# Attention stage in units of four tiles: running sum weighted on ScalarE, plain transposes in the residual, scattered rows based on GpSimd

## The reference

```python
def _L0_attn_ref(x, W_proj, A, Bp, D, W_delta, b_delta):
    delta, Bs, Cs, residual = jnp.split(x @ W_proj.T, 4, axis=-1)
    delta = jax.nn.softplus(delta @ W_delta.T + b_delta)
    dA = jnp.exp(delta * A[0, 0]) * Bp[0, :, 0]
    dB = jnp.cumsum(delta * Bp[0, :, 0], axis=1)
    uC = jnp.sum(x * Cs, axis=1, keepdims=True)
    Csum = jnp.sum(Cs, axis=1, keepdims=True)
    return dA * uC + dB * Csum + residual * D

x = x + 0.5 * ffn(layernorm(x))    # 32 experts, top 1, 640 slots each
x = x + _L0_attn_ref(layernorm(x))
x = x + 0.5 * ffn(layernorm(x))    # the same weights
```

## Time and profile before

| | |
|---|---|
| median of 3 runs | 1527.41 us (1524.95 to 1527.49) |
| the profiled execution | 1527.63 us |
| its span, first to last instruction | 1525.8 us |
| instructions | 31260 |
| mean granted TensorE clock over the span | 0.933 of full speed |
| busy share of the span | PE 85%, DVE 81%, ACT 71%, POOL 44% |
| HBM traffic over the span | 174 GB/s |

### The profile page before, as it was taken

One profiled execution on the slowest core, in us unless ns is written; L12 is line 12 of the kernel. 1 busy time (PEld: TensorE's weight loads), 2 busy tenths in 40 slices (PEclk: granted clock), 3 DMA queues, 4 the chain that ended last, 5 costly groups with the idle time before them and its releaser, 6 DMA issues. The chain is left out here.

```text
span 1525.8 us, 31260 instructions
## 1 busy us (share of the span) xinstructions
PE 1298.1 (85%) x10212; PEld 1229.3 (81%) x10215; DVE 1239.9 (81%) x3385; ACT 1088.4 (71%) x2343; POOL 675.9 (44%) x778
## 2 busy tenths in 40 slices
PE   5555029999999999799999999987639999999996
PEld 4334019999999999599888888986529999999996
DVE  8999408999999998388999999999837777777775
ACT  6778117777777775589889888886537777777773
POOL 0577752444334444222254554544633344434443
PEclk8877559999999999899999999999859999999999
DMA  9979546766667661921111232111144444444440
GB/s 325 346 271 378 198 160 206 234 223 227 232 207 234 218 212 61 291 72 35 36 62 53 73 102 84 47 60 53 54 144 128 125 148 129 145 147 130 148 130 25
DMA packets 149776, 234.74 MB, mean 154 GB/s; under 512 B 24333, under 2 KB 124390, under 8 KB 147568
## 3 DMA queue, kind: packets, MB, share of 16 engines
q1 hardware_dynamic: 121968, 188.24, 38.2%
q0 software_dynamic: 27648, 44.50, 8.5%
HBM read 128.51 MB, written 136.48 MB: 174 GB/s over the span
## 5 line engine op out<-in xcount | busy, mean ns | idle before, releaser
L1034 PE MATMUL ps<-xs,ws 128*128 128x320 f32 x3072 | 469.6, 311 | 2.2 <-issue 2.2
L1034 PEld LDWEIGHTS ps<-xs,ws 128*128 128x128 f32 x3072 | 454.7, 189 | 8.2 <-issue 8.2
L859 POOL DMA_INDIRECT slots_and_rows<-x x160 | 161.5, 1010 | 238.1 <-DVE x L976 198.5
L859 POOL DMA_INDIRECT out<-x x160 | 157.8, 987 | 236.5 <-DVE x L966 153.8
L1034 PE MATMUL ps<-ws,hs 128*128 128x256 f32 x1920 | 260.6, 289 | 1.3 <-DVE hs L955 1.3
L1034 PEld LDWEIGHTS ps<-ws,hs 128*128 128x128 f32 x1920 | 239.0, 190 | 1.7 <-DVE hs L955 1.7
L898 ACT ACTIVATE x<-x 128x256 f32<-128x256 f32 x320 | 165.0, 594 | 64.8 <-DMA x<-slots_and_rows 49.2
L880 ACT CAST xs<-ps 128x512 fp32r<-128x512 f32 (+1 forms) x192 | 98.3, 513 | 130.4 <-PE ps L1027 130.4
L987 DVE TENSOR_TENSOR hf<-ps,sg 128x320 f32<-128x320 f32 x256 | 124.6, 487 | 81.6 <-ACT sg L919 77.7
L948 DVE TENSOR_TENSOR xs<-ps,xs 128x512 fp32r<-128x512 f32 (+1 forms) x192 | 113.5, 592 | 72.5 <-ACT xs L880 72.5
L373 POOL DMA_INDIRECT slots<-x,slot x128 | 132.9, 1038 | 79.7 <-issue 43.7
(11 more groups left out here) (139 smaller groups left out, 2282.8 us busy)
## 6 DMA issues: line engine op xcount, KB each, us to landing
slots<-blank SPq DMA_DIRECT2D x16, 1310.0 KB
slots_and_rows<-blank SPq DMA_DIRECT2D x32, 655.0 KB, 4.8
x<-slots_and_rows SPq DMA_DIRECT2D x31, 655.0 KB, 3.9
x<-slots SPq DMA_DIRECT2D x31, 655.0 KB, 4.0
x<-slots_and_rows SPq DMA_DIRECT2D x32, 516.0 KB, 8.7
x<-in_x SPq DMA_DIRECT2D x32, 512.0 KB, 8.7
wraw<-in_w_gate SPq DMA_DIRECT2D x64, 256.0 KB
wraw<-in_w_up SPq DMA_DIRECT2D x64, 256.0 KB
```

Of the source, the lines that this page charges most:

```text
L859: nc.gpsimd.indirect_dma_start(out=rows, out_offset=bass.IndirectOffsetOnAxis(ap=factor(e, k, F_ID).bitcast(U32), axis=0), in_=XG[:, e % G ...
L1034: ins = pe.matmul(dst, left(a, k), right(b, k), start=(n == 0), stop=(n == len(terms) - 1))
```

## The change

In attention() the operations between delta and the residual handle four tiles (a unit m of two pairs, 512 columns for each half) in place of two:

- PSUM banks BZ[0] and BZ[1] now hold one half of the channels of a whole unit each, in place of one pair each. ACT's abs, exp, ln and DVE's softplus run once for each unit over twice the columns.
- A new ACT step, weight, multiplies the softplus by Csum times B and adds the bias term, into CS (which takes the room of the diagonals in the spare tile BLANK, and more). DVE's scan runs in place over CS, multiplying by one and adding; one half at the end of an odd step, the other at the start of the next. DVE's mix then multiplies the exponential by uC times B and adds the scan.
- The diagonals, the sign and size of uC and size_bias on ACT are removed. In residual the mixed tiles come back to rows by four plain transposes for each pair, ahead of the 12 matmuls.
- XS has five buffers in place of three. The lags are PLUS 3, RES 4, NEW (x_new, statistics) 5, BACK 5 (its evacuation one step later), LOGIT 7, BASE_AT 9, and all steps of post, count and scatter are two later. The first unit's rounding and softplus come ahead of the others. In an odd step PE does the residual before delta, in an even step behind it. ACT evacuates before d_a.
- GpSimd scales the tiles in place of ACT (pool_base) for the first seven batches; ACT keeps the last batch, and waits for GpSimd's bases before it.

```diff
+            def pool_base(self, pool, n):
+                t = n // NC
+                pool.wait_ge(self.turned.sem, self.turned.at(n + 1))
+                pool.wait_ge(self.scaled.sem, self.scaled.at(self.group_of[n] + 1))
+                apart(pool)
+                for j in range(CH):
+                    k = CH * n % TB + j
+                    x_t = self.stream.tile(CH * n + j)
+                    ins = nc.gpsimd.tensor_scalar(x_t, x_t, self.s1[:, t % RR, k:k + 1], self.s2[:, t % RR, k:k + 1],
+                                                  ALU.mult, ALU.add)
+                ins.then_inc(self.based.sem, 1)
...
                 t = n // NC
+                if self.own:
+                    act.wait_ge(self.based.sem, self.based.at(n))
...
+                QT, XB = 2 * CT, 5
...
-                XS = s([P, 3, 2, HC, CT], F32R)
-                AB = s([P, 2, HC, CT])
-                CC = s([P, 2, HC, CT])
-                YT = s([P, 2, HC, CT])
+                XS = s([P, XB, 2, HC, CT], F32R)
+                AB = s([P, 2, HC, QT])
+                YT = s([P, 2, HC, QT])
 
...
+                CS = SPARE[:, 0:2 * HC * QT].rearrange("p (a c d) -> p a c d", a=2, c=HC)
...
+                ONE1 = s([P, 1])
...
-                TURN, DELTA, PLUS, RES, BACK, LOGIT = 0, 1, 2, 3, 4, 5
+                TURN, DELTA, PLUS, RES, NEW, BACK, LOGIT = 0, 1, 3, 4, 5, 5, 7
                 A_NORM, GRAM = -8, -7
-                BASE_AT = 7
+                BASE_AT = 9
...
+                def soon(S, lag):
+                    return [n for n in range(NU) if n + lag - (3 if n < 2 else 0) == S]
+
+                def unit(S, lag):
+
+                    return [m for m in range(NU // 2) if 2 * m + lag == S]
+
+                def rounded(S):
+                    return [m for m in range(NU // 2) if 2 * m + (2 if m else -1) == S]
+
+                def summed(S):
+                    return [m for m in range(NU // 2) if 2 * m + (PLUS if m else 0) == S]
...
+                        for n in at(S, BASE_AT):
+                            if n < NU - NC:
+                                tail.pool_base(pool, n)
...
+                    def softplus(m):
+                        act.wait_ge(z_done.sem, z_done.at(2 * m + 2))
+                        if m >= 2:
+                            act.wait_ge(weighted.sem, weighted.at(m - 1))
+                        act.wait_ge(da_done.sem, da_done.at(m - 1))
+                        apart(act)
...
+                            ins = act.activation(AB[:, m % 2, h, :], ps[:, BZ[h], :], ACT.Abs, bias=BD[:, h:h + 1])
...
+                    def weight(m):
+                        a = 2 * m // NC
+                        act.wait_ge(factors.sem, factors.at(a + 1))
+                        act.wait_ge(softplus_done.sem, softplus_done.at(m + 1))
+                        act.wait_ge(scanned.sem, scanned.at(m))
+                        if m >= 2:
+                            act.wait_ge(mixed.sem, mixed.at(m - 1))
                         apart(act)
-                        act.activation(LB[:, a % 2, 0, :], UV[:, a % 2, 4, :], ACT.Ln).then_inc(size_links.sem, 1)
...
+                            ins = act.activation(CS[:, m % 2, h, :], AB[:, m % 2, h, :], ACT.Identity,
+                                                 bias=UV[:, a % 2, 2, h:h + 1], scale=UV[:, a % 2, 1, h:h + 1])
+                        ins.then_inc(weighted.sem, 1)
+
+                    def d_a(m):
+                        act.wait_ge(softplus_done.sem, softplus_done.at(m + 1))
+                        if m >= 2:
+                            act.wait_ge(residual_done.sem, residual_done.at(2 * m - 2))
+                        apart(act)
                         for h in range(HC):
-                            ins = act.activation(YT[:, n % 2, h, :], AB[:, n % 2, h, :], ACT.Exp,
-                                                 bias=LB[:, a % 2, 1, h:h + 1], scale=A1[:, h:h + 1])
+                            ins = act.activation(YT[:, m % 2, h, :], AB[:, m % 2, h, :], ACT.Exp,
+                                                 bias=ABD[:, h:h + 1], scale=A1[:, h:h + 1])
                         ins.then_inc(da_done.sem, 1)
...
-                        for a in batches(S, 2):
-                            size_bias(a)
-                        for n in at(S, PLUS):
-                            d_a(n)
+                        for m in unit(S, PLUS):
+                            weight(m)
                         for n in soon(S, TURN):
                             x_hi(n)
+                        for n in at(S, BACK + 1):
+                            tail.act_evac(act, n)
+                        for m in unit(S, PLUS):
+                            d_a(m)
                         for c in parts(S, [p[1] + 1 for p in POST_AT]):
                             tail.act_exp(act, c)
                         if A_NORM <= S < 0:
                             a_norm(S - A_NORM)
-                        for n in soon(S, DELTA):
-                            softplus(n)
+                        for m in rounded(S):
+                            softplus(m)
                         for n in at(S, LOGIT):
                             if n % 2 == 1:
                                 tail.act_keep(act, n // 2)
-                        for n in at(S, BACK):
-                            tail.act_evac(act, n)
                         for n in at(S, BASE_AT):
-                            tail.act_base(act, n)
+                            if n >= NU - NC:
+                                tail.act_base(act, n)
                         if S >= 0:
...
-                        dve.scalar_tensor_tensor(uv[:, 2, :], uv[:, 0, :], -1.0, uv[:, 0, :], ALU.mult, ALU.max)
...
-                        dve.tensor_tensor(uv[:, 3, :], uv[:, 1, :], uv[:, 6, :], ALU.mult).then_inc(f_links.sem, 1)
-                        for h in range(HC):
-                            ins = dve.tensor_scalar(DIAG[:, a % 2, h, :], IDENT, uv[:, 6, h:h + 1], None, ALU.mult)
-                        ins.then_inc(diag.sem, 1)
-                        dve.wait_ge(f_links.sem, f_links.next())
+                        dve.tensor_tensor(uv[:, 2, :], uv[:, 1, :], BD, ALU.mult).then_inc(factors.sem, 1)
...
+                    def softplus(m):
+                        dve.wait_ge(log_done.sem, log_done.at(m + 1))
                         for h in range(HC):
-                            ins = dve.scalar_tensor_tensor(AB[:, n % 2, h, :], ps[:, BZ[n % 2], h * CT:(h + 1) * CT],
-                                                           NBD[:, h:h + 1], AB[:, n % 2, h, :], ALU.max, ALU.add)
+                            ins = dve.scalar_tensor_tensor(AB[:, m % 2, h, :], ps[:, BZ[h], :], NBD[:, h:h + 1],
+                                                           AB[:, m % 2, h, :], ALU.max, ALU.add)
                         ins.then_inc(softplus_done.sem, 1)
...
+                    def scan(m, h):
+                        dve.wait_ge(weighted.sem, weighted.at(m + 1))
+                        dve.wait_ge(scanned.sem, scanned.at(m))
+                        apart(dve)
+                        start = 0.0 if 2 * m % NC == 0 else CS[:, 1 - m % 2, h, QT - 1:QT]
+                        ins = dve.tensor_tensor_scan(CS[:, m % 2, h, :], ONE1[:].to_broadcast([P, QT]), CS[:, m % 2, h, :],
+                                                     start, ALU.mult, ALU.add)
+                        if h == HC - 1:
+                            ins.then_inc(scanned.sem, 1)
+
+                    def mix(m):
+                        dve.wait_ge(scanned.sem, scanned.at(m + 1))
+                        dve.wait_ge(da_done.sem, da_done.at(m + 1))
                         apart(dve)
                         for h in range(HC):
-                            ins = dve.scalar_tensor_tensor(YT[:, n % 2, h, :], CC[:, n % 2, h, :],
-                                                           UV[:, n // NC % 2, 3, h:h + 1], YT[:, n % 2, h, :],
+                            ins = dve.scalar_tensor_tensor(YT[:, m % 2, h, :], YT[:, m % 2, h, :],
+                                                           UV[:, 2 * m // NC % 2, 0, h:h + 1], CS[:, m % 2, h, :],
                                                            ALU.mult, ALU.add)
                         ins.then_inc(mixed.sem, 1)
...
-                        for n in soon(S, PLUS):
-                            softplus(n)
+                        for m in unit(S, PLUS + 1):
+                            scan(m, 1)
+                            mix(m)
+                        for n in at(S, NEW):
+                            x_new(n)
+                        for n in at(S, NEW):
+                            dve.wait_ge(x_added.sem, x_added.at(n + 1))
+                            apart(dve)
+                            tail.dve_stats(dve, n)
+                        for m in summed(S):
+                            softplus(m)
                         chosen(S, 5, True)
```

(46 more changed lines are left out.)

90 lines of the change are left out of this document (23 added, 67 removed).

## The result

| | before | after |
|---|---|---|
| median of the executions shown | 1527.41 us | 1553.92 us (1552.31 to 1556.39) |
| ratio, 95% interval | 1 | 1.0186 (1.017 to 1.0203) |
| span of the profiled execution | 1525.8 us | 1550.5 us |
| DVE idle before the scan, waiting for ACT's weight | none | 57.9 us |
| DVE idle before the mix, waiting for ACT's d_a | 9.2 us | none |

The changed kernel is 26.5 us slower. The forecast was 1551 us, 2.9 less than measured. In the kernel after, the scan is L1410, the mix L1420, softplus on DVE L1401, x_new L1428, x_lo L1394, ACT's weight L1301, its logarithm L1290, delta L1524, the residual L1534 and L1540, and GpSimd's base L407.

The account below looks back on a forecast made before the run. DVE was taken as the bound, 7.0 us a pair. Terms 9.9 - 6.3 (factors) + 4.2 + 2.5 + 6.0 + 3.9 + 3.7 = +23.9 us on 1527.6 gave 1551 us, range 1526 to 1574.

Parts of the forecast that it names:

- DVE bounds, and the weight's wait is new: Attention stage: DVE is the bound; between softplus and scan it newly stands still 1.70 us for ACT's weight, 31 places.
- DVE's own work: DVE's softplus, scans and mix per two-pair unit: 7.04 us with the new wait against 6.71, +9.9 us over 30 units.
- x_new on the residual: DVE's x_new waits 0.35 us for PE's residual in about 12 units without post work in the even step: +4.2 us.
- The Gram sums in batch 1: DVE's a_sums waits for PE's Gram sums in batch 1, where no post work covers it: +2.5 us.
- DVE held by GpSimd: GpSimd's bases beside DVE's scans and mixes hold DVE 0.2 us for each unit: +6.0 us (0 to 24).
- The rival with the full price: Every second DVE scan or mix meets a GpSimd base, 0.8 us a unit, not 0.2: 1570 us, chance 0.10.
- the second rival: GpSimd's queue becomes the bound from 1.35 us for each base; at 1.7 us a base, 1580 us; chance 0.07.
- Start: Filling of the stage: Gram-sum copy 3.5 us later, factors -0.9, weight +1.5; the first x_new about +3.9 us later.
- The end: GpSimd's scatters bound the end; DVE reaches slots of batch 6's second half +3.7 us later, the 43.9 us behind unchanged.
- That PE was the bound: PE's queue sets the 14.0 us; its shorter residual takes 24 us off, 1504 us; chance 0.12.
- The clock rival: Granted clock at 0.94 all through the stage, slow PE stretches costing DVE 20 to 30 us: 1575 us, chance 0.05.
- rival 4: Savings cancel weight's wait with the factors' part, bases and Gram sums cost nothing: about 1528 us, chance 0.08.

Follow-up runs that it names:

- e2: The changed kernel without ACT's weight, DVE's scan reading softplus's output itself (weighting left out of the result): 1514.82 us, 0.9913 of before.
- e4: The changed kernel with one more ACT activation of 512 columns ahead of weight's two: 1576.27 us, 1.0319 of before.
- e11: The changed kernel with weight signalling behind each half, and each half's scan waiting for its half alone: 1535.32 us, 1.0058 of before.
- e3: The changed kernel with the bases of all batches back on ACT, none on GpSimd: 1549.29 us, 1.0144 of before.
- e1: The changed kernel with DVE's softplus moved ahead of x_new and its statistics: 1541.42 us, 1.0094 of before.
- e5: e1 with delta ahead of the odd residual in PE's step: 1529.35 us, 1.0015 of before.
- e12: e5 with odd steps' Gram sums moved behind the next even step's delta, and e11's signals for each half: 1513.69 us, 0.9924 of before.

## Why the prediction was right, step by step

- **DVE bounds, and the weight's wait is new.** Right, and shown by dose (e2, e4, e11). Predicted: 1.70 us in 31 places, 52.7 us; measured 1.81, 56.1 us. The 0.11 is the way to ACT, which takes 0.12 us behind softplus and not 0.04, and DVE's start behind it.
- **DVE's own work.** Softplus's group has a mean of 0.739 us (0.74 expected), scans at 1.28 (1.25), scan to scan and scan to mix 1.20 and 1.45 (1.19 and 1.43), mix 1.33 (1.33). So the fixed costs of half the instructions were saved as worked out, and the slope taken from the bf16 scan was near: 256 more columns cost the fp32 scan 556 ns (medians 727 and 1283), not 517.
- **x_new on the residual.** Predicted 0.35 us in 12 places, 4.2 us; measured 0.24 to 0.26 in 8 places, 2.0 us. The other two of the ten places in the view lie outside this term: 1.58 us is the first x_new itself, in the fill, and 2.14 stands at 1116.40, behind batch 6's slots. The residual is also shorter than taken, 1.87 us from its first transpose to the next matmul (PE's rows at 668.75 and 670.62), not 2.03. **The Gram sums in batch 1:** 2.5 predicted; 2.9 us in two places, one of 2.7.
- **DVE held by GpSimd.** 6.0 us taken, between 0 and 24. e3 bounds it: 4.6 us for all that the bases do. The mean of the scans tells 64 x (1307 - 1265) ns = 2.7 us of it, the mix's next to nothing. The rival with the full price (1570 us) is refuted. (That such instructions get in each other's way, as the Trainium skill states, SBUF — State Buffer, Who interferes with whom, is seen in rows such as 948.20 and 948.86. That the first one runs its whole length undisturbed and the other one stands until then, as the same section has it, isn't seen in them: that scan starts first and still takes 0.37 us more, and the seven scans that start 0.14 us behind a base lose 0.20 us of the 0.41 that the two share. The spans shown for GpSimd are rough. The price made from the rule for every unit doesn't come out.) Ten lengthened scans make 2.4 us of it, the rest of the 4.6 isn't found in rows. Why it is so little: only 14 of the 56 pairs of bases meet one of these scans, and where a base is lengthened it ends 0.2 to 0.4 us behind the scan, mostly with the scan as short as ever.
- **GpSimd's base, 0.8 taken between 0.45 and 1.7.** Median 554 ns, mean 676; the lower bound was the nearer one. With all of it gone from the queue (e3) only 4.6 us go, so the second rival (1580 us) falls.
- **Start, the term that was mis-sized.** Set against the stage's start, which in the profiled execution of after is 2.5 us earlier (its first factor operation at 619.89, before at 622.39), the copy of the Gram sums comes 639.41 - 638.09 + 2.5 = 3.8 us later (3.5 predicted). The first x_new comes 654.57 - 649.90 + 2.5 = 7.2 us later, 3.9 predicted. What I left out is what PE and ACT do while the copy is late. PE's timeline of after:

```profile
640.02 0.33 PE L1499 MATMUL ps<-cf,a 128*128 128x128 f32 x1 [2.93 <-DVE a L1369]
...
641.16 1.21 PE L1487 MATMUL ps<-a 128*128 128x257 f32 x2
...
643.88 0.78 PE L1513 MATMUL ps<-cf,a 128*128 128x128 f32 x4
```

  PE stands for 2.93 us, and behind that the granted clock is 0.60 in the mean between 640 and 644 us, mostly the lower of its two levels, 1.2 GHz (before, in the same 4 us, 1.00): 2 Gram matmuls take 1.21 us and not 0.60, and the next turn is only at 643.88. ACT rounds that turned pair (x_hi) before it does the first weight, whose factors DVE had ready at 642.85 (ACT's timeline, then DVE's last row of the factors):

```profile
644.70 0.58 ACT L1276 CAST a<-ps 128x512 fp32r<-128x512 f32 x1 [4.67 <-PE ps L1513]
645.18 1.10 ACT L1269 ACTIVATE a<-x,a 128x256 f32<-128x256 f32 x2
646.17 1.51 ACT L1301 ACTIVATE blank<-a 128x512 f32<-128x512 f32 x2
```

```profile
642.69 0.16 DVE L1390 TENSOR_TENSOR a<-a,vec 128x2 f32<-128x2 f32 x1
```

  The prediction put the weight behind softplus and the factors alone. In ACT's queue it stands behind x_hi and a norm of the next batch (1.10 us), and x_hi behind PE's slowed Gram, so weight starts 646.17 - 642.85 = 3.3 us behind its factors. That the 3.3 us between 3.9 and 7.2 are these is read from the rows; no run tried it.
- **From the first x_new to the slots of batch 6.** 432.1 us before, 454.4 after: +22.3, and the prediction's terms between them make 9.9 - 6.3 + 4.2 + 2.5 + 6.0 + 3.7 = 20.0. The waits that were larger (3.4 on the weight, 0.4 on the Gram sums) less what was smaller (2.2 on the residual, 1.4 for the bases) would make 20.2; 2.1 us more were found, and which term holds them stays open.
- **The end.** POOL's timeline of after, from the scatters behind batch 6's slots to the last one, and one row of before:

```profile
1109.93 1.22 POOL L373 DMA_INDIRECT slots<-x,slot  x1 [4.93 <-DVE slot L542]
...
1150.66 0.97 POOL L373 DMA_INDIRECT slots<-x,slot  x1 [0.31 <-issue]
```

```profile
1105.19 0.97 POOL L373 DMA_INDIRECT slots<-x,slot  x1 [1.44 <-ACT x L407]
```

  41.7 us from first to last, where the earlier trace rows has 42.9, with 32 scatters in both (the prediction counts 33). The prediction took this as unchanged and without a gap; before had one of 1.44 us, for a base of ACT, and after has none over 0.31. The sum of what was found: -2.5 + 7.2 + 22.3 - 1.2 = +25.8, against +24.7 between the spans; the last 1.1 us lie behind the scatters. Set against the forecast's +23.9, start and weight were priced too low (3.3 and 3.4 us), residual, bases and end too high (2.2, 1.4 and 1.2), and the stage began 2.5 us earlier in this execution: that the total comes so near is in part luck.
- **The rivals.** That PE was the bound (1504 us) is refuted by after itself: PE's residual fell by more than the 0.74 us for each unit (2 x (2.40 - 1.87) = 1.06) and the time didn't. It had a point, though. With the wait away PE's queue and the ring through it come next (e1, e5, e12), which fits with e12 standing at 1513.7 and not lower. The clock rival took hold only in the fill; elsewhere the granted clock is 1.00 and 0.93, before 1.00 and 0.94.
- **The signs of being wrong.** DVE's wait before the scan is 1.81 us, not under 1. From x_new to x_new a unit takes 15.0 us over the four units of a late batch (943.49 to 1003.46), not under 14.0; only units without routing work are at 12.2.
- **Slips in the working.** The forecast's own bounds add up to about 1575 us at the upper end, not 1570; GpSimd's queue is 12.0 us for each unit, not 12.1; and the 11 us that rival 4 takes off aren't worked out from anything. None of them moves the forecast.

## What to carry to other kernels

Before work goes from the bounding engine to another, write down what the bounding engine does between handing its data over and asking for them back: if nothing stands there, each round trip costs its whole length, and the saved instructions have to pay for it. Here 12.6 us could be had (e2), and 57.9 us of waiting were bought with them. Then cover the round trip in all queues at once: DVE's order alone gave 12.5 us, PE's alone cost 10.2, both with the odd steps' Gram sums moved gave 37.5, and a signal for each half 18.6 by an edit of three lines. And merging two pairs' work into one instruction also merges their buffers: the bank that was two in turn became one, and the ring through it makes DVE's largest wait in the best version (15.1 us in e12).

## What the runs showed of the hardware that was not expected

- GpSimd's tensor_scalar with two pointer operands takes 554 ns in the median for 128x256 fp32, and up to 2.5 us; 112 of them cost the kernel at most 4.6 us, while 0.8 us for each unit, 24 us, had been thinkable.
- The granted clock was 0.60 in the 4 us behind one gap of 2.9 us on PE at the stage's start, while the stretch from 878 to 934 us, in which PE is idle 7.7 of 56 us in short gaps, stays at 1.00.
- An instruction's start behind another engine's signal took 0.12 us (DVE to ACT) and 0.17 us (ACT to DVE) in a plain unit; a round trip with 1.52 us of work costs 1.81.
